# A two-layer GRU with a mixture of experts behind it: one-bank steps moved to slots 4 and 12, projections shifted, state copies halved

## The reference

```
mixed = tanh(x @ W_in.T + b_in + context)
h1 = gru(mixed)            # 1024 dependent steps, state of 256
h2 = gru(h1)               # again 1024 dependent steps
x  = x + ((1 + sigmoid(gate)) * h2) @ W_out.T + b_out
# one GRU step
r = sigmoid(xr + hr);  z = sigmoid(xz + hz);  n = tanh(xn + r * hn)
h = (1 - z) * n + z * h
```

## Time and profile before

| what | value |
| --- | --- |
| median of 3 runs | 2240.25 us (2235.08 to 2249.32) |
| the profiled execution | 2236.78 us, span 2235.0 us |
| granted TensorE clock in it | 0.998 |
| TensorE busy (matmul) | 2078.5 us, 93% of the span |
| TensorE weight load | 1521.4 us, 68% |
| VectorE | 1858.4 us, 83% |
| ScalarE | 1198.0 us, 54% |
| GpSimd | 543.5 us, 24% |

### The profile page before, as it was taken

The page is one execution under the profiler, slowest core; times in us unless marked ns, Lnnn a source line. Parts: engine busy times, 40 slices in busy tenths (PEclk is TensorE's granted clock), DMA queues, the critical chain, the costliest instruction groups (busy, mean ns, idle before and its releaser), DMA issues.

```text
span 2235.0 us, 163118 instructions
## 1 busy us (share of the span) xinstructions
PE 2078.5 (93%) x70480; PEld 1521.4 (68%) x70480; DVE 1858.4 (83%) x11225; ACT 1198.0 (54%) x6471; POOL 543.5 (24%) x2414
## 2 busy tenths in 40 slices
PE   6988889999999999999999999999999998999986
PEld 3656666677666776766766676666767776777765
DVE  4888888888888888988889888888888888988874
ACT  2555555555555555555555555555555555555541
POOL 1222222222222222222222222222222222222220
PEclk9999999999999999999999999999999999999999
DMA  5000000000000000000000000000000000000000
GB/s 214 4 5 5 5 5 5 23 5 5 10 5 23 5 5 9 5 24 5 5 10 5 23 5 9 5 24 5 5 9 23 5 10 4 5 22 9 5 16 18
DMA packets 10882, 32.82 MB, mean 15 GB/s; under 512 B 1368, under 2 KB 6832, under 8 KB 9136
## 3 DMA queue, kind: packets, MB, share of 16 engines
q1 hardware_dynamic: 10160, 22.38, 2.8%
HBM read 20.22 MB, written 2.16 MB: 10 GB/s over the span
## 4 chain that ended last, share of the span: by engine, by line
PE 56%; DVE 28%; ACT 11%; issue 3%; DMA 0%; SPq 0%; DVEq 0%
PE bank L334 25%; PE bank L326 17%; PE bank L273 11%; DVE n_first L402 10%; DVE cells L422 7%; ACT factors L467 6%; ACT cells L471 4%; DVE r_pre L393 4%; DVE z_pre L403 3%; PE bank L307 3%; DVE bank L411 2%; DVE n_second L378 1%; DVE bank L377 0%; DVE x L666 0%; PE bank L636 0%
## 5 line engine op out<-in xcount | busy, mean ns | idle before, releaser
L334 PE MATMUL bank<-w_h,cells 128*22 128x128 f32 (+4 forms) x32768 | 1373.3, 280 | 35.0 <-issue 14.7
L334 PEld LDWEIGHTS bank<-w_h,cells 128*22 128x22 f32 (+4 forms) x32768 | 870.9, 110 | 133.5 <-DVE cells L422 87.6
L326 PEld LDWEIGHTS bank<-w_h,cells 128*22 128x22 f32 (+4 forms) x28672 | 547.5, 112 | 539.7 <-DVE cells L422 502.0
L326 PE MATMUL bank<-w_h,cells 128*22 128x64 f32 (+4 forms) x28672 | 796.0, 224 | 101.3 <-DVE cells L422 75.8
L508 POOL TENSOR_SCALAR cells<-cells 128x4 f32<-128x4 f32 x2048 | 463.4, 226 | 1638.0 <-DVE cells L422 1634.8
L461 ACT ACTIVATE n_second<-r_pre 128x4 f32<-128x4 f32 x2048 | 426.7, 208 | 499.8 <-DVE r_pre L393 458.9
L467 ACT ACTIVATE factors<-z_pre 128x4 f32<-128x4 f32 x2048 | 429.6, 210 | 490.8 <-DVE z_pre L403 411.7
L402 DVE STREAM_TRANSPOSE n_first<-bank 128x64 f32<-128x64 f32 x2048 | 597.3, 292 | 54.7 <-PE bank L334 42.3
L422 DVE TENSOR_TENSOR_SCAN cells<-factors,cells 128x18 f32<-128x18 f32 x2048 | 394.2, 192 | 239.6 <-ACT cells L471 166.0
L393 DVE STREAM_TRANSPOSE r_pre<-bank 128x64 f32<-128x64 f32 x2048 | 481.5, 235 | 37.7 <-PE bank L326 26.3
L403 DVE STREAM_TRANSPOSE z_pre<-bank 128x64 f32<-128x64 f32 x2048 | 427.0, 208 | 0.1
(11 more groups left out here) (87 smaller groups left out, 531.9 us busy)
## 6 DMA issues: line engine op xcount, KB each, us to landing
c_all<-weights SPq DMA_DIRECT2D x6, 1024.0 KB
x_t<-in_x_t SPq DMA_DIRECT2D x4, 512.0 KB, 7.5
w_1e<-in_w_1e SPq DMA_DIRECT2D x1, 2048.0 KB
w_2e<-in_w_2e SPq DMA_DIRECT2D x1, 2048.0 KB
w_x<-in_w_x SPq DMA_DIRECT2D x2, 768.0 KB, 8.1
w_h<-in_w_h SPq DMA_DIRECT2D x2, 768.0 KB, 9.7
w<-in_w SPq DMA_DIRECT2D x3, 512.0 KB
out_y<-y SPq DMA_DIRECT2D x6, 256.0 KB, 3.8
```

The source lines that it names most:

```text
L326: mm = pe.matmul(r_sums[l][p][32 * g:32 * g + B * (j + 1)], state_tile(l, j, kt), w_h[l][:, kt, g, 2 * U:], start=False, stop=False, tile_ ...
L334: mm = pe.matmul(sums[l][p][32 * g:32 * g + B * (j + 1), 0:width], state_tile(l, j, kt), w_h[l][:, kt, g, 0:width], start=False, stop=Fals ...
```

## The change

The one-bank steps move from slots 6 and 14 to slots 4 and 12, for both layers. Layer 0's first projection half moves from slot 10 to slot 4. Layer 1's projections move one slot ahead, to slots 0 and 1, and VectorE takes them apart in two goes, r in slot 1 and n in slot 2. In slot 1 VectorE has no mixture operation in part 1 any more. GpSimd copies the first half of a chunk's states at step 8 of the chunk and the rest at the start of the next chunk, there ahead of layer 0's halving; `dve_h` waits for the copying at step 8 and not at step 0.

```diff
 def r_first(l, j):
-    return (j + LAG * l) % 8 != 6
+    return (j + LAG * l) % 8 != 4
 def projection_pieces(l):
-    return {10: 0, 12: 1} if l == 0 else {1: 0, 2: 1}
+    return {4: 0, 12: 1} if l == 0 else {0: 0, 1: 1}
 ...
-        return (j, part) in ((13, 0), (2, 1)) or self.sparse and part == 1
+        return (j, part) in ((13, 0), (1, 1), (2, 1)) or self.sparse and part == 1
 ...
-        def take_x(v, l, p):
+        def take_r(v, l, p):
             v.tensor_copy(r_sums[l][p], sums[l][p][:, 2 * U:3 * U])
+        def take_n(v, l, p):
             v.transpose(n_second[l][p][:, :, :, 2].rearrange("p i b -> p b i"),
                         blocks(sums[l][p][:, 3 * U:])).then_inc(sets[l][1 - p]["xn"], 1)
 ...
-            if j == 0:
+            if j == CH // 2:
                 v.wait_ge(s["pool"], 1)
 ...
+                if CH <= s < T + CH and j == 1:
+                    v.wait_ge(sets[1][p]["x"], 1)
+                    take_r(v, 1, 1 - p)
                 if CH <= s < T + CH and j == 2:
-                    v.wait_ge(sets[1][p]["x"], 1)
-                    take_x(v, 1, 1 - p)
+                    take_n(v, 1, 1 - p)
 ...
-        def copy_states(pool, to, l, done):
-            pool.tensor_copy(to[:, :, 0:ROWS - B], held(l)[:, :, B:])
+        HALF = ROWS // 2
+        def copy_first(pool, to, l):
+            pool.tensor_copy(to[:, :, 0:HALF], held(l)[:, :, B:HALF + B])
+        def copy_second(pool, to, l, done):
+            pool.tensor_copy(to[:, :, HALF:ROWS - B], held(l)[:, :, HALF + B:])
             pool.tensor_copy(to[:, :, ROWS - B:], held(l)[:, :, 0:B]).then_inc(done, 1)
 ...
+                if s <= T and j == 0:
+                    pool_await(pool, 0, s)
+                    copy_second(pool, stage[1][:], 0, sets[0][p]["pool"])
                 if t0 is not None:
+                    if j:
+                        pool_await(pool, 0, t0)
                     pool_half(pool, 0, t0)
+                    if j == CH // 2:
+                        copy_first(pool, stage[1][:], 0)
 ...
                 if t1 is not None:
+                    pool_await(pool, 1, t1)
                     pool_half(pool, 1, t1)
+                    if t1 % CH == CH // 2:
+                        at = (t1 + CH // 2) * B
+                        copy_first(pool, hist[:, :, at:at + ROWS], 1)
```

More of the change, by code:

```diff
@@ L439, in dve_slots @@
                         v.wait_ge(sets[0][p]["x"], 1)
-                        take_x(v, 0, 1 - p)
+                        take_r(v, 0, 1 - p)
+                        take_n(v, 0, 1 - p)
                 mixture_at(v, "dve", s, 0, base)
@@ L497, in act_slots, with pool_await @@
                 mixture_at(act, "act", s, 1, base)
-        def pool_half(pool, l, t):
+        def pool_await(pool, l, t):
             p, j = t // CH % 2, t % CH
@@ L507, in pool_half @@
                 pool.wait_ge(sets[l][1 - p]["h"], CH)
+        def pool_half(pool, l, t):
+            p, j = t // CH % 2, t % CH
             pool.tensor_scalar(cell_part(step_rows(l, j), 3), cell_part(step_rows(l, j), 1), 0.5, None, ALU.mult)\
                 .then_inc(sets[l][p]["for_h"], 1)
-        def copy_states(pool, to, l, done):
-            pool.tensor_copy(to[:, :, 0:ROWS - B], held(l)[:, :, B:])
+        HALF = ROWS // 2
[3 more added lines that the diff above has]
+            pool.tensor_copy(to[:, :, HALF:ROWS - B], held(l)[:, :, HALF + B:])
             pool.tensor_copy(to[:, :, ROWS - B:], held(l)[:, :, 0:B]).then_inc(done, 1)
@@ L527, in pool_slots @@
                 p = c % 2
+                if s <= T and j == 0:
+                    pool_await(pool, 0, s)
+                    copy_second(pool, stage[1][:], 0, sets[0][p]["pool"])
                 if t0 is not None:
+                    if j:
+                        pool_await(pool, 0, t0)
                     pool_half(pool, 0, t0)
[L530 to L535, removed]
+                    if j == CH // 2:
+                        copy_first(pool, stage[1][:], 0)
+                    if j == 0:
                         if c % (TB // ROWS) == TB // ROWS - 1 and c < T // CH - 1:
@@ L540, in pool_slots @@
                 if t1 is not None:
+                    pool_await(pool, 1, t1)
                     pool_half(pool, 1, t1)
+                    if t1 % CH == CH // 2:
+                        at = (t1 + CH // 2) * B
+                        copy_first(pool, hist[:, :, at:at + ROWS], 1)
                     if t1 % CH == 0:
                         now = sets[1][t1 // CH % 2]["pool"]
-                        copy_states(pool, hist[:, :, t1 * B:t1 * B + ROWS], 1, now)
+                        copy_second(pool, hist[:, :, t1 * B:t1 * B + ROWS], 1, now)
                     for mix in mixtures:
@@ L552, in pool_slots @@
                     pool.wait_ge(sets[1][1]["h"], CH)
-                    copy_states(pool, hist[:, :, T * B:T * B + ROWS], 1, s_hist)
+                    copy_second(pool, hist[:, :, T * B:T * B + ROWS], 1, s_hist)
                     pool.wait_ge(s_hist, 1)
@@ L894, in _ @@
             v.wait_ge(s_x0, 1)
-            take_x(v, 0, 0)
+            take_r(v, 0, 0)
+            take_n(v, 0, 0)
             run(v, dve_slots)
```

## The result

The changed kernel took 2214.54 us in the median of four runs (2213.11 to 2216.89), the kernel before 2239.48 (2235.08 to 2249.32): a ratio of 0.9884, 95% interval 0.985 to 0.9918. The profiled execution of after took 2216.89 us, span 2215.1, against 2236.78 and 2235.0. So about 20 to 25 us were gained. On another chip, where the kernel before took 2220.67, the ratio was 0.9907 (0.989 to 0.9925).

A forecast was written before the change was run, and what follows sets the result against it. TensorE was taken to wait for the state, each slot lasting one trip around a layer. Terms of -0.41 us a chunk, cut to -0.36, gave -20 us: 2217 profiled, median 2218, range 2204 to 2243.

The forecast's parts named there:

- The sum by stretch: Whole run: -0.36 us a chunk over 49.5 chunks up to slot 792, -17.8 us, and -2.2 us behind; together -20 us.
- the signs that I had named: Changed trace: slot lengths, bias and GpSimd waits that would show the forecast; slots 5, 13 above 2.03 or stalls past 40 refute.
- One-bank steps leave 6 and 14: Slots 6 and 14 become ordinary, from 2.21 and 2.17 to 1.95 us; -0.48 us a chunk.
- a wait that I described and priced at nothing: Slot 6, layer 1: the one-bank step's wait for ScalarE's bias write gets 0.2 us of cover; no term in the sum.
- They come to 4 and 12: Slot 4 goes from about 1.95 to 2.17 us, slot 12 from 2.11 to 2.17; +0.22 and +0.06 us a chunk.
- The projection leaves 10: Slot 10 falls from 2.11 to 1.95 us, -0.16 a chunk; one-bank slots 4 and 12 hide the projection with 0.06 cover.
- Layer 1's x in two goes: Slot 3: the r turn comes 0.12 us earlier; bounds nothing to 0.10, taken as -0.05 us a chunk.
- GpSimd, 0: Slots 0 and 8: copies ahead of the halving stay hidden with 0.18 us to spare, step 8's copy costs nothing; 0.
- the port rule: GpSimd reading SBUF fully blocks a two-input VectorE instruction; the forecast said the row disagrees, 0.04 us a chunk at most, left at 0.
- The slower rival: Slots 0, 8 of layer 0, 3, 11 of layer 1: copies hold up VectorE's scans; +0.44 us a chunk, 2265 us; 10%.
- The stalls on issue: Instruction fetch: the change moves the stalls, not their number; as rival "Nothing" 5 to 15 us lost, about 2235 us; 7%.
- The late stretch: Last 14.5 chunks: about half the slots bound by TensorE at 2.20 us, so half the gain, 0.15 a chunk, -2.2 us.

The follow-up runs named there:

- e1: The kernel before with the one-bank steps alone moved to slots 4 and 12; 2218.56 us, ratio to before 0.9917.
- e3: The kernel before with one-bank steps in slots 4 and 12 and layer 0's projection in 4 and 12, the rest as before; ratio to before 0.9903.
- e2: The kernel before with layer 0's first projection half alone moved from slot 10 to slot 4; ratio to before 1.0013.
- e4: The kernel before with layer 1's projection in slots 0 and 1 and x taken in two goes, copies as before; ratio to before 0.9983.
- e5: The kernel before with GpSimd's state copies by halves alone, and the copy wait at step 8; ratio to before 1.0006.
- e8: The changed kernel with 16 small matmuls ahead of the slots, putting later TensorE instructions 64 records further on; 2205.95 us, ratio to before 0.993.
- e7: The changed kernel with no one-bank step, every step having two products; 2230.29 us, ratio to before 1.0045.

## Why the prediction came out

The direction and size came out: forecast -20 us in the profiled execution (2236.78 to 2217), measured -19.9 (2216.89); forecast median 2218, measured 2214.54, a ratio of 0.9884 where I had leaned to within 1%. (By my own 3.5 us between profiled execution and median the 2218 should have been 2220 or 2221.) The sum by stretch was -17.8 up to slot 792 and -2.2 behind; measured -20.3 up to slot 784 and +0.3 behind. Its steps did less well than its total: of the latency in the sum about half at most is found, and a term that I had put at nothing filled the hole. That the total came out so near is in good part luck.

Of the signs that I had named, slots 6, 10 and 4 (1.96, 1.98 and 2.13), the stalls on issue (34.9 us), slots 5 and 13 (1.96 and 1.99) and slot 6 without a wait for the bias held. Slots 14 and 12 missed by 0.02 (2.00 and 2.20), slot 3 stands at 2.02 where I wanted less, and TensorE does wait for GpSimd three times in slot 0.

**One-bank steps leave 6 and 14, -0.48.** Slots 6 and 14 went from 2.14 and 2.17 (medians) to 1.96 and 2.00: -0.35. My slot 6 of 2.21 was the long one of its kind. Slot 7 gave 0.10 more, which I hadn't counted (2.06 to 1.96, and the same in e1). The likely cause is that in slot 6 layer 1 no longer waits for the bias write, a wait that I described and priced at nothing; slot 15, behind a one-bank slot without such a wait, kept its 2.02. In the waits of before it stands with 20 cases, all in slot 6, and in those of after there is none:

```profile
PE bank L334 <- ACT bank L473: 7.0, 20, 0.4
```


**They come to 4 and 12, +0.28.** 2.01 to 2.13 and 2.12 to 2.20: +0.20. Right in kind, and 0.08 too much.

**The projection leaves 10, -0.16, and is hidden.** -0.14, and hidden by 0.05 to 0.06 us. Right as a mechanism, but e3 against e1 shows next to no time for it. Slot 11 rose by 0.13 at the same time, but only 0.04 of it comes with the projection: in the quiet chunks slot 11 has 1.94 before and in e1, and 1.98 in e2 and e3. The likely reason is that before, layer 1 was ahead after the long slot 10, and now both layers come in step. In slots 152 to 791 e1 has 2.08 with the projection still in slot 10, so the rest comes with the one-bank steps. Part of it are stalls on issue (in these slots 11 0.4 us before, 2.0 after, 3.8 in e3); beyond that the cause stays open.

**Layer 1's x in two goes, -0.05.** Slot 3 -0.03, e4 -3.8 us in all. Near, though e4's medians don't show where the 3.8 us come from.

**GpSimd, 0, and the weighing of the port rule.** In sum right (e5: 1.0006). Slots 1 and 2, priced at 0, rose by 0.04 and 0.03; they do so in e5, with the copies alone (1.98 and 2.01), and not in e4 (1.94 and 1.98). But I said that the row disagrees with a full block, and that was too quick. In slot 11, layer 1's new first copy starts on the same instant as layer 0's scan. GpSimd of the changed kernel there:

```profile
463.24 0.23 POOL L525 COPY hist<-cells 128x32 f32<-128x32 f32 x1
```

and VectorE:

```profile
463.24 0.29 DVE L414 TENSOR_TENSOR_SCAN bank<-n_first,n_second 128x12 f32<-128x12 f32 x1
```

The scan has 0.29 us where 0.19 is usual. Of these scans (line 411, 414 after) 71 are above 0.22 us after and 43 before, of 2048 each; all that they take beyond 0.195 is 3.9 us against 2.8. After, 30 of them stand in slot 11, where before had none; 28 of the 43 of before stand in slot 0, beside the old copies, and I had read only a single one. In the quiet chunks slot 11 has 2.03 us where e3 has 1.98, which may be this. In slots 152 to 791 it isn't what makes slot 11 long: with a long scan the median is 2.07, without one 2.11. So the Trainium skill (SBUF — State Buffer, Who interferes with whom) has the direction right: such a scan is held up when GpSimd reads beside it. The trace shows 0.10 us for a copy of 0.23, not the whole copy, where the two start together. The slower rival needed 0.2 us on every copy.

**The stalls on issue, priced at nothing.** This is where the sum failed though the total held. I put the issue stalls among the rivals as something that moves only its place. They shrank. The medians of a chunk fell by 0.15 us (32.44 to 32.29), and those of the quiet chunks by 0.18, where I had -0.36. The mean fell by 0.42: about 0.27 us a chunk, 13 us in 48 chunks, came from fewer and shorter disturbances. The 13 us are of one pair of profiles and rough: e2 against e3 gives the same 0.30 of 0.46 us, but e5 against e8, which differ by the same one-bank steps and both projections, only 0.08 of 0.31. By the times, e1 gains 16 us where its quiet chunks give 7. So between a quarter and two thirds of the gain isn't latency; a closer split isn't shown.

A stall looks like this in the kernel before, slot 13, TensorE: the matmuls of one step break off, nothing is waited for, and the rest follows 0.46 us later.

```profile
570.86 0.39 PE L334 MATMUL bank<-w_h,cells 128*28 128x128 f32 x5
571.71 0.54 PE L334 MATMUL bank<-w_h,cells 128*28 128x128 f32 x10 [0.46 <-issue]
```

The profile shows what is missing. It has the transfers that bring TensorE's instructions, one of 16 KB for every 256 of its 141,424 (70480 matmul records, as many weight loads, and its waits). In part 3 of the page, queue, packets, MB and share:

```profile
q8 instruction: 552, 9.04, 1.7%
```

Numbered from 0 in order of time, 117 of the 206 gaps of the weight loads above 60 ns, with 43.0 of their 52.7 us, come at number 193 or 194 of a block of 256; after it is 102 of 200, with 34.4 of 43.8 us. In e8, where every instruction stands 64 further on, 74 of 158 are at 193 or 194 again. At these gaps the weight loads go on 1.40 us (median; 90% between 1.24 and 1.59) after the end of the transfer that came last, and in none of the 551 blocks of the kernel before does number 194 start less than 1.20 us after the end of its own. In the stall above the transfer runs from 569.25 to 570.13, and the weight loads go on at 571.71. So a gap is a block of instructions that comes late: a transfer takes 1.10 us (median), with the 1.40 some 2.5 us, and it starts only about 190 instructions ahead of number 194 (medians: 191 where there is no gap, 162 where there is one).

From these numbers one can estimate when it binds. A slot of two products in each layer has 128 TensorE instructions and 16 more with a mixture operation, 144 in 1.96 us, so some 184 in 2.5 us: just short of 190. A projection adds 16 more. A slot with a one-bank step in both layers has 64 fewer, some 110 in 2.5 us. That is the rest which a one-bank slot gives the supply, and the traces show it. In slots 152 to 791 of the kernel before, 45 of 101 block borders in slots 4, 5, 12 and 13 have a gap, and 3 of 63 in slots 6, 7, 14 and 15, the one-bank slots and those behind them. In the changed kernel it is 2 of 80 and 4 of 81, and in e7, with no one-bank step, 35 of 93 and 27 of 90. In the other eight slots gaps became more frequent, 61 of 179 where it was 31 of 176: they moved, and together shrank from 30.6 to 21.5 us.

By slot, before, slots 5 and 13 had 9.3 and 6.9 us of these gaps, the last ones ahead of the one-bank slots; after, 0.2 and 0.0. (Slot 10 has more, 11.3 and 11.8, mostly from the loads of `c_all` described at the end.) e7 shows that without one-bank steps the stalls double and the kernel loses over 1%. Why the last slots ahead of the new places, 3 and 11, are hit less than 5 and 13 were, stays open.

The Trainium skill (Runtime: NRT & Kernel Launch, Instruction fetch mechanics) has TensorE's instructions refilled in blocks of 256, and the trace agrees; it also says that fetching is hidden behind issue, and here 22.5 to 57.5 us of waits say that it isn't always.

**The late stretch, -2.2.** Measured +0.3. The step failed, and no run takes it apart. In slots 800 to 1022 the medians of slots 5 and 6 fell (2.06 to 1.95 and 2.15 to 1.96), but those of slots 2 and 3 rose by 0.14 and 0.13, and the gaps on issue above 60 ns from slot 792 on were 16.1 us before and 18.4 after. So something was gained there too and taken back; that these slots are bound by TensorE at 2.20 us, as I had said, isn't shown.

## What to carry to other kernels

When a kernel of 141,000 straight-line TensorE instructions waits on "issue", count instructions as a resource beside latency: look whether the gaps come at the same place of every 256 instructions, and how many instructions a slot issues in the time that a block takes to arrive. Compare the median of a repeated stretch with its mean; if they differ, part of any change's effect will be in the difference. Two delays that each wait for something else can share one slot, but first look which chain sets the slots behind it: a slot that had slack from its neighbour loses it. A wait that is always met already, on a chain of dependent steps, is not free: 0.07 us here.

## What the runs showed that I had not expected

A broadcast of 1 MB into all partitions can hold up the transfer of TensorE's instructions. In the kernel before, `c_all` is loaded at 393 GB/s up to 698 us, and in the next 2 us TensorE is busy for 0.07 us:

```profile
696.00:698.00 2.00, 2.00 (x73) 1.28 (x64) 1.64 (x11) 1.08 (x7) 0.46 (x2) 1.00 0.95 393
698.00:700.00 2.00, 0.07 (x1) 0.00 (x0) 0.20 (x1) 0.21 (x2) 0.23 (x1) 1.00 0.04 12
```

(columns: stretch, length, busy us of TensorE, weight load, VectorE, ScalarE, GpSimd with counts, granted clock, DMA share, GB/s). The transfer of the next instructions starts at 698.06, just behind the last large packet of the broadcast (698.03), and one instruction ahead of the place where the block is needed, where others start about 190 ahead. It takes 0.88 us, and TensorE goes on at 700.28, 1.35 us behind its end. The load at 1230 us does the same (a gap of 2.5 us), the others cost 1.3 us or less each in this profile. Near the nine loads of `c_all` of a run, six of them of 1 MB, the gaps above 60 ns add up to 9.1 us before and after; the change didn't touch this.

The chips also differ in the kernel before itself, 2234.92 on one and 2221.95 and 2220.67 us on the others, and so do the issue waits: 34.9 and 22.6 us for the changed kernel in its two profiles. Small changes of such a kernel can only be compared on one chip, with the kernel before beside them.
